# A thought's large weights as half-precision parts: split once, stored, fetched again; other rings and another order

## The reference, cut to what matters

```python
def ffn(x):                               # called on layernorm(x); twice
    x_norm = layer_norm(x, in_gamma, in_beta)
    thought = x_norm[:, -1, :] @ agg_w + agg_b          # one row per sequence
    for _ in range(4):
        t = layer_norm(thought, pn_gamma, pn_beta)
        t = gelu(t @ d1_w + d1_b)                       # 1024 x 4096
        thought = thought + (t @ d2_w + d2_b)           # 4096 x 1024
    broadcast = (thought @ bc_w + bc_b)[:, None, :]
    out = x + sigmoid(x @ gate_w + gate_b) * broadcast
    return layer_norm(out, out_gamma, out_beta)

x = x + 0.5 * ffn(layernorm(x))
x = x + attention(layernorm(x))           # blocks of 128 tokens: own block and the one before,
x = x + 0.5 * ffn(layernorm(x))           # squared relu of the scores, then w_o
```

## Time and profile before

| | us |
|---|---|
| three runs | 2334.28, 2327.05, 2333.17 (median 2333.17) |
| the profiled execution, its own time | 2312.91 |
| its span | 2311.6 |
| PE busy | 2174.6 (94%) |
| DVE busy | 1054.9 (46%) |
| ACT busy | 464.4 (20%) |
| POOL busy | 485.7 (21%) |
| moved by DMA | 488.58 MB, 211 GB/s over the span |

### The profile page before, as it was taken

How to read it: one execution, slowest core, us unless ns; L and a number is a source line. 1 busy time by engine, 2 the same in 40 slices (tenths; PEclk the granted TensorE clock), 3 DMA queues, 4 the chain that set the end, 5 groups by cost and what they waited for, 6 DMA issues and landing times.

```text
span 2311.6 us, 29856 instructions
## 1 busy us (share of the span) xinstructions
PE 2174.6 (94%) x12384; PEld 1096.7 (47%) x12384; DVE 1054.9 (46%) x2021; ACT 464.4 (20%) x716; POOL 485.7 (21%) x409
## 2 busy tenths in 40 slices
PE   8978999999999879999999989999999998999996
PEld 3423333343433356655455544556545664445443
DVE  2421012444433344444244334425334424999998
ACT  0013002222222122211211111211111212322331
POOL 0000000000000132221122111212112202666665
PEclk9989999999999989999999999999999999999998
DMA  7279857968798612237786695685774225222221
GB/s 310 100 254 370 301 183 266 371 256 330 283 340 312 247 66 94 77 140 266 278 289 211 232 337 192 227 318 210 291 267 170 84 73 200 92 91 93 100 83 55
DMA packets 112133, 488.58 MB, mean 211 GB/s; under 512 B 10544, under 2 KB 10752, under 8 KB 95232
## 3 DMA queue, kind: packets, MB, share of 16 engines
q1 hardware_dynamic: 112000, 486.69, 57.0%
HBM read 406.94 MB, written 79.71 MB: 211 GB/s over the span
## 4 chain that ended last, share of the span: by engine, by line
PE 84%; DMA 9%; DVE 3%; issue 2%; POOL 1%; SPq 1%; ACT 1%; DVEq 0%; ACTq 0%; POOLq 0%
PE product_banks L721 56%; PE product_banks L752 9%; DMA thought_weights<-in_d_w 6%; PE thought_acc L908 5%; PE thought_acc L901 5%; PE product_banks L847 5%; PE turn_banks L730 3%; DVE bn_parts L1074 1%; DMA wide_b<-x_scratch 1%; DMA wide_a<-in_w_attn 1%; PE thought_turn L916 1%; POOL arena L1430 0%; DMA arena<-in_x 0%; DMA arena<-gate_scratch 0%; POOL stats L1389 0%
## 5 line engine op out<-in xcount | busy, mean ns | idle before, releaser
L721 PE MATMUL product_banks<-gate_arena,arena 128*128 128x512 f16 x1536 | 350.4, 381 | 0.0
L721 PE MATMUL product_banks<-gate_arena,wide_a 128*128 128x256 f16 x3072 | 344.2, 273 | 1.6 <-DVE gate_arena L1087 1.6
L721 PE MATMUL product_banks<-wide_b,gate_arena 128*128 128x512 f16 x1536 | 343.1, 379 | 0.0
L721 PE MATMUL product_banks<-wide_a,arena 128*128 128x512 f16 x1536 | 337.9, 380 | 0.0
L721 PEld LDWEIGHTS product_banks<-gate_arena,wide_a 128*128 128x128 f16 x3072 | 299.2, 98 | 64.2 <-issue 29.6
L721 PEld LDWEIGHTS product_banks<-gate_arena,arena 128*128 128x128 f16 x1536 | 145.2, 98 | 219.9 <-issue 62.9
L721 PEld LDWEIGHTS product_banks<-wide_b,gate_arena 128*128 128x128 f16 x1536 | 146.3, 98 | 208.5 <-issue 43.2
L752 PE MATMUL product_banks<-wide_a,wide_b 128*128 128x512 f32 x512 | 234.0, 607 | 9.3 <-DMA wide_a<-in_w_attn 8.6
L721 PEld LDWEIGHTS product_banks<-wide_a,arena 128*128 128x128 f16 x1536 | 150.7, 98 | 175.3 <-issue 1.6
L1095 DVE SCALAR_TENSOR_TENSOR arena<-product_banks,inverse_gate,arena 128x512 f32<-128x512 f32 x128 | 96.0, 751 | 239.5 <-PE product_banks L721 239.2
L1389 POOL TENSOR_TENSOR token_stats<-stats,minus_half 128x1 f32<-128x1 f32 x64 | 62.7, 979 | 588.2 <-DVE stats L1081 571.3
(11 more groups left out here) (126 smaller groups left out, 1786.9 us busy)
## 6 DMA issues: line engine op xcount, KB each, us to landing
thought_weights<-in_d_w SPq DMA_DIRECT2D x256, 1024.0 KB, 6.8
arena<-in_x SPq DMA_DIRECT2D x64, 512.0 KB, 8.2
x_scratch<-arena SPq DMA_DIRECT2D x64, 512.0 KB, 6.4
gate_scratch<-arena SPq DMA_DIRECT2D x32, 512.0 KB, 9.1
arena<-gate_scratch SPq DMA_DIRECT2D x32, 512.0 KB, 7.8
arena<-x_scratch SPq DMA_DIRECT2D x32, 512.0 KB, 6.0
wide_b<-x_scratch SPq DMA_DIRECT2D x32, 512.0 KB, 3.3
out<-wide_b SPq DMA_DIRECT2D x32, 512.0 KB, 2.6
```

Source lines behind the costliest of these rows:

```text
L721: mm = pe.matmul(bank, left(i, k), right(j, k), start=(n == 0), stop=(n == 3 * KD - 1))
```

## The change

What is computed stays the same, to the rounding of the parts.

1. The weights are handled in units of 128 x 1024 (512 KB). Aggregate, broadcast and the whole first step of the first thought (`t_whole`, `t_whole_top`) stay float32. In that first step ACT also sums the magnitudes in each row of each d1 and d2 unit (`ACT.Abs` with a sum output); DVE makes the scales of these sums once, in `t_scales`.
2. From the first thought's second step on, a unit is scaled and split: ACT writes the high part (`t_high`), DVE the remainder (`t_low`), both half precision, together 512 KB. The thought's values are divided by the scales and cut into three bfloat16 parts (`t_parts`), six stationary columns instead of two. A unit is then four half-precision products of 512 columns in the four strips. Units with odd k are split in the first thought's second step and stored in memory (`parts_dram`); units with even k are split anew in its second, third and fourth step, and once more, and then stored, in the second thought's first step. All other uses fetch the stored pairs (`t_pair`). In numbers: 160 splits, 64 of them stored, 288 fetched pairs.
3. d1 is done in four products of 1024 columns instead of two of 2048, so sums are turned 44 times instead of 28; the turn is now four products of the sums, as stationary operand, with a small matrix that adds the strips (`sum_whole`, `sum_parts`).
4. Slots: four for loads, four for split units, in the first thought also the two halves of `thought_row`; in the second thought from its second step on, eight for pairs.
5. Beats: `paced_on` takes lists of pieces; the paces are 0.75 in the first fold, 0.9 in the three early gate tiles, 1.2 in the second fold, 1.16 in the gate tiles, 0.95 in stage 2. `LATE` is 4.
6. The splits of the three big matrices: ACT rounds the high part one row ahead (`round`), DVE makes the low part. The gate rows are taken without rests between the maxima; x(0) is fetched with them, x(1) and x(2) after the splits.
7. The arena has 13 tiles: gates 2, rows 3, one value slot and one weight slot fewer for odd tiles; the last gate bias lies in the gate arena. The stores of a group's results stand before the next group's first q piece instead of behind it.

The core of the diff:

```diff
-X_RING, PAIR_RING, GATE_RING, FOLD_RING, ROW_RING, W_RING = 3, 2, 3, 2, 4, 3
-PREP_RING, XS_RING, X3_RING, H3_RING = 2, 3, 8, 5
+X_RING, PAIR_RING, GATE_RING, FOLD_RING, ROW_RING = 3, 2, 2, 2, 3
+PREP_RING, XS_RING, X3_RING, H3_RING, GATE3_RING = 2, 3, 8, 5, 3
-EARLY, LATE = 3, 2
+EARLY, LATE = 3, 4
+PACES = (0.75, 0.9, 1.2, 1.16, 0.95)
...
+FOR_LOADS, FOR_SPLITS, FOR_FIRST = [0, 1, 2, 3], [4, 5, 6, 7], [8, 9]
...
+    def load(self, tau, step, matrix, k, c, how, used):
+        n = len(self.loads)
+        slots = FOR_LOADS + (FOR_FIRST if tau == 0 else FOR_SPLITS if step else [])
+        slot = slots[n % len(slots)]
...
+    def how(tau, step, matrix, k):
+        if matrix in ("agg", "bc"):
+            return "whole"
+        if tau == 0 and step == 0:
+            return "top"
+        if k % 2:
+            return "keep" if (tau, step) == (0, 1) else "pair"
+        return "split" if tau == 0 else "keep" if step == 0 else "pair"
...
+            if s[0] == "unit":
+                j = mine.index(s[1]) + ahead
+                beat += [("high", mine[j])] if j < len(mine) else []
+                beat += [("low", mine[j - 1])] if j - 1 < len(mine) else []
...
-        out.insert(1, ("x2_stores", n - 1))
+        out.insert(0, ("x2_stores", n - 1))
...
+def rounded_ahead(m, fetches):
+    out = [("round", m, 0)]
+    for k in range(KD):
+        out += ([("round", m, k + 1)] if k + 1 < KD else []) + [("split", m, k)] + fetches[k:k + 1]
+    return out
...
-    gate_rows = [("gate_rows",)] + [("rest",)] * 3
-    for k in range(KD):
-        gate_rows += [("gate_max", k), ("rest",)]
+    gate_rows = [("gate_rows",), ("x", 0)] + [("rest",)] * 3
+    gate_rows += [("gate_max", k) for k in range(KD)]
...
-    out += paced([p for n in range(TILES - LATE, TILES) for p in plan_gate(n)], plan_prep(0), 1.3, PE_PIECES)
+    out += paced([p for n in range(TILES - LATE, TILES) for p in plan_gate(n)], plan_prep(0), 0.9, PE_PIECES)
...
+            elif kind in ("t_unit", "t_pair"):
...
+                stationary = thought_parts[:, scaled_at(matrix, k, c) % KH, :]
+                for part in range(2):
+                    for h in range(HALVES):
+                        at = PE_COLS * (2 * part + h)
+                        mm = pe.matmul(thought_acc[at:at + PARTS * B, :], stationary,
+                                       unit[:, part, h * BANK:(h + 1) * BANK], start=first, stop=last)
+                mm.then_inc(unit_used, 1)
...
-                for s in range(PER):
-                    mm = pe.transpose(thought_turn[:, s * P:(s + 1) * P], t_wide[:, s * P:(s + 1) * P],
-                                      identity[:, :])
+                for s in range(PER):
+                    mm = pe.matmul(thought_turn[:, s * HALVES * B:(s + 1) * HALVES * B], t_wide[:, s * P:(s + 1) * P],
+                                   sums[:, :], start=True, stop=True)
...
+            elif kind == "t_high":
...
+                act.activation(parts_at(split.slot)[:, 0], unit_at(load.slot), ACT.Copy,
+                               scale=unit_scale[:, at:at + 1]).then_inc(unit_high, 1)
...
+            elif kind == "t_low":
...
+                dve.wait_ge(unit_high, n + 1)
+                dve.scalar_tensor_tensor(out=parts_at(split.slot)[:, 1], in0=unit_at(load.slot),
+                                         scalar=unit_scale[:, at:at + 1], in1=parts_at(split.slot)[:, 0],
+                                         op0=ALU.mult, op1=ALU.subtract).then_inc(unit_low, 1)
```

579 lines of the change are left out of this document (400 added, 179 removed).

## The result

| | before | after |
|---|---|---|
| runs beside each other, median | 2331.22 us | 2358.87 us |
| their range | 2327.05 to 2334.28 | 2355.43 to 2366.44 |
| ratio, 95% interval | | 1.0124, 1.0093 to 1.0155 |
| the profiled execution | 2312.91 us | 2366.44 us |
| its span, mean granted clock | 2311.6, 0.983 | 2365.2, 0.971 |

The change made the kernel 1.2% slower, 29 us on the scale of the runs. The forecast was 89 us faster; 2244 missed by 115.

What follows compares the result with a forecast made beforehand. PE was taken to bound the kernel nearly everywhere, with cover on ACT and DVE. The terms -72 + 12 - 17 - 22 - 18 + 28 summed to -89 us, giving 2244 us at the runs' scale, range 2215 to 2275.

Steps and rivals of the forecast that it cites:

- the products of the thought: Both thoughts: 448 half-precision units at 0.33 us and 48 float32 chunks, 194.8 instead of 266.6 us, -72 us.
- turning the sums: Turns of the thought's sums: 44 at 0.56 us instead of 28 at 0.44, +12 us.
- hole before the gates: Before the first gate tile: PE's waits for ACT's normalised tile and lower clock, 21 us, shrink by 17.
- late hole: From the first thought's end to the first query product: 18.9 us idle and about 4 of clock, -22 us.
- DMA waits: Second thought: 12.5 + 10.5 us of waits behind a ring of three chunks, -18 us with eight slots.
- what is put under cover: New sums, roundings, remainders and stores on ACT, DVE and SP's queue, thin in four places: +28 us.
- The test that I had named for them: Sign of being right, for the thought's products: the rows of thought_acc together under 200 us.
- the places: Thin cover in the first thought: step 0 +12 (to 25), step 1 +11 (to 35), steps 2 and 3 +3 (to 40).
- C: Rival, slower: turnover of six slots in the first thought sets the pace; at 14 us turnover, 2354 us; chance 0.06.
- My signs of being wrong: Serial strips; gate-run waits over 30 us; clock under 0.95 at 150 to 350 us; second thought's DMA waits over 10 us.
- -10 if DVE's hold reaches PE: End of the first thought: only -10 us instead of -22 if DVE, held at the first prep sum, delays PE.

Runs made afterwards that it cites:

- e6: Changed kernel with only 8 units split and stored, all other half-precision units fetching these pairs (wrong weights, same bytes): 2279.13 us, ratio 0.9792 to the kernel before.
- e1: Changed kernel with the whole thought left in float32, its slots, order, 44 turns and LATE kept, paces refitted: 2347.43 us, ratio 1.0085 to the kernel before.
- x6: Changed kernel with the 64 sums of magnitudes of step 0 on 16 of 1024 columns: 2358.81 us, ratio 1.011 to the kernel before.
- x7: Changed kernel with the thought all float32 and one product per turn of sums instead of four: 2319.44 us, ratio 0.9945 to the kernel before.
- e3: Changed kernel with two units per beat, so half the entries into the strips, paces refitted: 2416.01 us, ratio 1.0383 to the kernel before.
- x1: Changed kernel with roundings and remainders of the 160 splits on 16 of 1024 columns, all waits, stores and fetches kept: 2315.26 us, ratio 0.9949.
- x2: Changed kernel with all 160 splits made but only the first 8 kept units stored, pairs fetched from those: 2348.44 us, ratio 1.0081.
- x5: Changed kernel with roundings and remainders on 16 columns and only the first 8 kept units stored: 2294.02 us, ratio 0.9836.
- e2: Changed kernel with all 64 units split once and stored in the first thought's step 1, 64 splits not 160, more slots for pairs: 2307.09 us, ratio 0.9907.
- b1: Changed kernel with 64 splits, all stored, step 1 slower, later steps faster, big matrices' splits and first preparation later, rests added: 2291.77 us, ratio 0.985.

## Why the prediction was wrong, by its own steps

| step of the sum | forecast | measured | by |
|---|---|---|---|
| the products of the thought | -72 | -71 | e6 against e1 (-68), which has no sums of magnitudes (x6, 3) |
| turning the sums | +12 | +23 | 44 x 0.81 - 28 x 0.44; x7 |
| hole before the gates, late hole, DMA waits | -57 | about -3 | e1's +20 less the turns' 23, so in the float32 frame |
| what is put under cover | +28 | about +80 | e6 (77), x6 (3) |
| sum | -89 | +29 | the runs |

**The products** were right, in mechanism and size: 0.32 us per unit, of which 0.10 are the entry into the strips (e3). The test that I had named for them was badly chosen: PE's rows of `thought_acc` sum to 237 us, not under 200, since a unit is busy for 0.39 us while its distance is 0.32, and some of them stood in the lower clock.

**What is put under cover** is the step that failed, and with it the result. Three errors were in it. I counted the six load slots and wrote that ten units are in hand when a product begins; but a unit is handed to PE through the four slots for split parts, and one slot's turn holds, one behind the other, the rounding (1.14 us), a place in DVE's queue and the remainder (1.31), PE's use and, for kept units, a store (5.3 us median to landing). I added ACT's and DVE's time as shares of a tile, 17 us of DVE beside PE's 15, and took the average for cover: both engines are in order, and each eviction or moment ahead of a remainder is a wait of PE where nothing is in hand. And I bounded the places at 25, 35 and 40 us but took 12, 11 and 3. The measured loss is 63 us under the gate tiles (after against e6), where I had 14, and some 20 in stage 2 (1124.6 against 1103.5 us), where I had 2, but there two single profiles of one kernel differ by 8. The three early tiles grew from 90.9 to 99.4 us although their hole shrank; ACT's sums have 5 us of that stretch and 3 of the whole (x6), and the weights came at 336 GB/s instead of the 416 of the term. In the list of rivals it was C's kind of mechanism, a turnover that sets the pace, and its price (2354 us) is near the result by luck: it stands on a turnover of 14 us, which was chosen, and C put it in the loads' six slots. The runs put it in the roundings, remainders and stores (x1, x2, x5), of which 67 of 77 us are shown, and ACT's waits put it in the split slots. C had got 6 in 100, with a condition (13.3 us of turnover) that I had not tested on the other ring.

My signs of being wrong mostly missed this. PE waits 17.9 us for remainders in the gate run, under the 30 that I had named, since DVE's full queue shows as late copied sums and scaled input too; the clock between 150 and 350 us is 0.97, not under 0.95. Only the DMA waits of the second thought (over 10 us) came true.

**The turns** were mis-sized: I priced four products at four times a lone one. The row of a lone product is one behind a longer product. Four in a row are 0.14 + 3 x 0.22. The trace shows two weight loads of 128 x 128 float32 for each such product (280 for the 35 turns of split parts), 195 ns each:

```profile
L1135 PEld LDWEIGHTS thought_turn<-sum_parts,t_wide 128*128 128x128 f32 x280 | 36.1, 195 | 15.0 <-DVE t_wide L1641 10.4 <-issue 3.1
```

In the turn at 1571.44 the eight loads are busy for 0.97 us, which overlap and so start (0.97 - 0.195) / 7 = 0.11 us apart. A turn by transposes, before, has the same stationary operand but one load each, four in 0.47 us (mean 144 ns), also 0.11 apart, and its four take 0.44. So both forms cost 0.11 us per load, and a product has two: that is why four products take twice the time of four transposes. That it is the load which holds PE is read from these rows; no run changed the load alone.

**The hole before the gate tiles** shrank from 12.46 + 4.43 to one of 5.00 us, as said in the step (12 of 17 us).

**The end of the first thought** failed on the branch that I had named, "-10 if DVE's hold reaches PE": 11.1 us of idle time are left of 18.9. DVE stands in `prep_y` (L1433) for POOL, with tile 30's moments behind it; ACT's normalised tile comes late and PE waits. In the trace of after:

```profile
816.71 3.28 DVE L1433 TENSOR_TENSOR arena<-arena 128x1024 f32<-128x1024 f32 x1 [6.46 <-POOL arena L1730]
820.02 1.29 DVE L1333 BATCH_NORM_STATS2 bn_parts<-arena 128x6 f32<-128x512 f32 x2
...
821.99 1.97 PE L936 MATMUL turn_banks<-identity,arena 128*128 128x128 f32 x8 [7.43 <-ACT arena L1201]
```

**The DMA waits of the second thought** stayed, 19.1 us of 23.0: 12.5 on stored pairs and 6.6 on the aggregate's first unit, where I took 18 off. I gave a fetch 18 us to land, on average; it lands in 5.6 (median). What holds its issue, the free slot or SP's other waits ahead of it, was not tried.

That leaves some 15 us: the two holes gave about 20 us of idle time by the rows, and e1 has its frame, without turns, at only -3. Its float32 chunks still wait 22 us for DMA (38 before), and the waits of L1052 that name nobody are 8 us longer (30.4 against 22.7). What eats the rest was not settled; e1's interval alone is plus or minus 7.

The clock is a part of the loss, 18 of the 63 us in the gate run, and goes with the holes: it is at 1.00 in e6's gate run (4.5 us idle), at 0.97 in that of after (49) and at 0.92 in that of e3 (81). No run changed the clock by itself.

## What to carry to other kernels

Before work is put "under cover" of PE, write down the ring through which its result reaches PE: how many slots, and what stands in one slot's turn, in series, each with its queue. The shares of busy time say only that it fits on average; with in-order engines and nothing in hand each of them is late by what stands ahead of it. Where something costly is made from fixed data, make it once, early and slowly, and fetch it later (e2 and b1, with more slots for the pairs, turned a loss of 1.2% into gains of 0.9% and 1.5%). And price a run of short products by the loads of their stationary operands, counted in the trace, not by a lone product.

## What was not expected of the hardware

- A float32 product against few columns takes 0.14 us behind a long product and 0.22 us behind another such one: such a product has two loads of its 128 x 128 stationary operand in the trace, a transpose one, and in a row both forms come to 0.11 us per load.
- Two shortenings in one slot's turn, 41 and 10 us alone, gave 67 together (16 more than the sum, plus or minus 13).
- Halving ACT's work in the three early tiles (77 to 39 us) moved the DMA share from 0.91 to 0.95 and the stretch by 5 of 99 us: a second bound lay a few per cent behind the first.
- Two profiled executions of one kernel differ by 11 us, 8 of them in stage 2, with granted clocks of 0.983 and 0.975.
